# Two attention layers and two expert layers on one core: scores by array tiles of 32 rows, a new order around them, grouped row sums and reordered final adds

## The reference, cut to what matters

```
L0 attention:  q, k, v = x W + b, rotary on q and k, 16 heads of 8 channels
               softmax(q k^T / sqrt(8)) v, then Wo
L0 experts:    8 experts, each takes the 256 tokens with its highest probability
L1 attention:  q from x, k and v from a latent of 32 channels, 16 heads of 8
L1 experts:    16 experts, each token takes its best 4: weights softmax(top 4)
               sum over the 4 of  w * (gelu(x W1 + b1) W2 + b2)
```

## Time and profile before

| | us |
|---|---|
| median of three runs | 691.19 |
| the profiled execution | 691.12 |
| its span in the profile | 689.3 |
| PE busy / DVE busy / ACT busy / POOL busy | 540.6 / 493.6 / 385.9 / 326.8 |
| granted clock of TensorE, mean over the span | 0.882 |

### The profile page before, as it was taken

How to read it: one execution, slowest core, us unless ns; L and a number is a source line. 1 busy time by engine, 2 the same in 40 slices (tenths; PEclk the granted TensorE clock), 3 DMA queues, 4 the chain that set the end, 5 groups by cost and what they waited for, 6 DMA issues and landing times.

```text
span 689.3 us, 15558 instructions
## 1 busy us (share of the span) xinstructions
PE 540.6 (78%) x4528; PEld 388.7 (56%) x4528; DVE 493.6 (72%) x1779; ACT 385.9 (56%) x1004; POOL 326.8 (47%) x431
## 2 busy tenths in 40 slices
PE   4769999998512895378999999823899999999960
PEld 2224555555301785244555555512777899999960
DVE  6788888995576421868888899587577778863257
ACT  2348888886200564256888888530344555566633
POOL 5665555505001577562333330734344677777630
PEclk9689999999755799589999999955799999999985
DMA  6502080001100125336404000103334455555572
GB/s 185 160 1 71 9 232 24 1 1 41 26 0 3 39 49 101 122 94 178 136 11 123 1 2 1 47 16 105 119 126 136 156 185 177 177 194 203 199 249 77
DMA packets 64437, 65.08 MB, mean 94 GB/s; under 512 B 16115, under 2 KB 45955, under 8 KB 63846
## 3 DMA queue, kind: packets, MB, share of 16 engines
q1 hardware_dynamic: 57094, 52.49, 23.9%
q0 software_dynamic: 7264, 11.62, 6.9%
HBM read 29.77 MB, written 11.87 MB: 60 GB/s over the span
## 4 chain that ended last, share of the span: by engine, by line
PE 58%; DVE 22%; issue 6%; DMA 4%; POOL 4%; SPq 3%; ACT 2%; DVEq 0%; ACTq 0%; POOLq 0%
PE bank L1285 10%; PE bank L1296 9%; PE bank L898 8%; PE bank L865 8%; PE bank L881 7%; DVE mx L1687 2%; DVE passed L1887 2%; PE bank L915 2%; PE bank L1239 2%; PE bank L1080 1%; POOL rstd L711 1%; POOL sum L766 1%; PE bank L1266 1%; DVE keys L1737 1%; DVE stats L1831 1%
## 5 line engine op out<-in xcount | busy, mean ns | idle before, releaser
L1687 DVE TENSOR_REDUCE mx<-bank 128x2 f32<-128x512 f32 x256 | 166.2, 686 | 32.2 <-PE bank L865 29.3
L1406 ACT ACTIVATE prob<-bank 128x512 f32<-128x512 f32 x256 | 141.4, 597 | 45.4 <-PE bank L881 34.7
L1587 ACT ACTIVATE queries<-bank,prob 128x128 f32<-128x128 f32 x316 | 90.1, 368 | 81.3 <-PE bank L1285 80.5
L865 PE MATMUL bank<-keys,queries 128*128 128x512 f16 x256 | 99.3, 402 | 9.6 <-DVE queries L1747 4.0
L1285 PE MATMUL bank<-keys,prob 128*128 x632 | 90.0, 287 | 3.8 <-ACT keys L1579 3.7
L881 PE MATMUL bank<-QT,keys 128*128 128x256 f16 x512 | 90.3, 276 | 0.0
L1296 PE MATMUL bank<-W,queries 128*128 x632 | 87.8, 283 | 0.0
L1285 PEld LDWEIGHTS bank<-keys,prob 128*128 128x128 f32 x632 | 79.7, 198 | 8.8 <-issue 7.0
L779 POOL DMA_INDIRECT prob<-xs,idx_g x64 | 61.5, 961 | 46.4 <-DVE idx_g L2118 27.8
L1296 PEld LDWEIGHTS bank<-W,queries 128*128 128x128 f32 x632 | 77.6, 193 | 2.0
L898 PE MATMUL bank<-prob,augs 128*32 128x256 f32 x1024 | 77.2, 389 | 0.0
(11 more groups left out here) (272 smaller groups left out, 1021.4 us busy)
## 6 DMA issues: line engine op xcount, KB each, us to landing
prob<-W SPq DMA_DIRECT2D x79, 258.0 KB
W<-in_w SPq DMA_DIRECT2D x48, 256.0 KB, 3.5
sum<-zero SPq DMA_DIRECT2D x3, 1024.0 KB, 8.8
xr<-XT SPq DMA_DIRECT2D x12, 128.0 KB, 2.0
xs<-X SPq DMA_DIRECT2D x2, 768.0 KB, 6.2
prob<-xs,idx_g POOLq DMA_INDIRECT x80, 2.7
XB<-sum SPq DMA_DIRECT2D x1, 1024.0 KB, 5.3
Y<-sum SPq DMA_DIRECT2D x4, 256.0 KB, 4.8
```

The lines of the kernel that those rows point to most:

```text
L865: nc.tensor.matmul(bank[S1B[u % 2]][:, :], QT[par][:, j, P * qt:P * qt + P], KB[par][:, j, 2 * qp:2 * qp + 2, :], start=True, stop=True).t ...
L1406: nc.scalar.activation(prob[:, v % 8, :, :], st_bank(b, v)[:, :], ACT.Exp, scale=SCALE).then_inc(exp_done, 1)
L1587: last = nc.scalar.activation(hid2[:, p % 4, f, :], bank[2 + p % 2][:, P * f:P * f + P], ACT.Gelu, bias=wc[:, p % 4, WB + f:WB + f + 1])
L1687: nc.vector.tensor_reduce(m_at, bank[S1B[u % 2]][:, :].rearrange("p (j k) -> p j k", j=2), AX.X, ALU.max).then_inc(s1_used, 1)
```

## The change

- **Scores by row tiles.** `KB` goes. Keys are kept once, in `keyT`. A score matmul takes as operands only the 32 partitions of its head. `s1` is now two matmuls of 256 columns (heads of the same q in two groups) into one bank; unit u has q = u % 4. `st` is still two of 256.
- **Key evacuation by ACT alone**, two copies of 128x512 instead of four of 32x512 on ACT and four on DVE; one semaphore `kt_ready`. The memsets of `KB` go.
- **Order.** `soft_units`, and the places of `bt`, `av`, `front_proj`, `out_transposes`, `query_transposes` and `key_transposes` on PE; the matching places on ACT and DVE. `output_statistics` moves behind `m_ready`.
- **Experts of layer 1.** The expert number is computed once for each pair in the source. The sum L2130 is done for eight tiles at once.
- **Final adds.** Slice 1 to Y, bias to X, Y to X, then wait for slice 2 and add it to X.

```diff
 def soft_units(u):
-    return {2: [0, 1], 3: [2], 4: [3], 5: [4], 6: [5], 7: [6], 8: [7], 9: [8], 10: [9], 12: [10, 11],
-            14: [12], 15: [13]}.get(u, [])
+    return {2: [0], 3: [2], 4: [3], 6: [4, 5], 7: [6], 8: [7], 9: [8], 10: [9], 11: [10], 12: [11],
+            14: [12, 13]}.get(u, [])
...
 def s1(lay, i, par, u):
-    qt, j, qp = u // 8, (u % 8) // 2, u % 2
+    qt, jp, q = u // 8, (u % 8) // 4, u % 4
+    rows = slice(HP * q, HP * q + HP)
...
-    nc.tensor.matmul(bank[S1B[u % 2]][:, :], QT[par][:, j, P * qt:P * qt + P],
-                     KB[par][:, j, 2 * qp:2 * qp + 2, :], start=True, stop=True).then_inc(s1_done, 1)
+    for j in range(2):
+        last = nc.tensor.matmul(bank[S1B[u % 2]][:, L * j:L * j + L], QT[par][rows, 2 * jp + j, P * qt:P * qt + P],
+                                keyT[par][rows, 2 * jp + j, :], start=True, stop=True)
+    last.then_inc(s1_done, 1)
...
 def st(lay, b, par, v):
-                                KB[par][:, j, q, P * kt:P * kt + P], QT2[:, j, :],
+                                keyT[par][rows, j, P * kt:P * kt + P], QT2[rows, j, :],
...
 def pe_iteration(lay, i, par, soft_on, front_on, tail_on):
-        bt(lay, i - 2, 0)
     for u in range(16):
         s1(lay, i, par, u)
+        if u == 1 and tail_on:
+            bt(lay, i - 2, 0)
...
+        if u == 3 and soft_on:
+            st(lay, i - 1, nxt, 1)
...
+        if u == 7 + late and proj_on:
+            front_proj(lay, i + 2, par, 1)
+        if u in (10, 12) and soft_on:
+            av(lay, i - 1, nxt, 1, u // 12)
+        if u == 13 and tail_on:
             out_transposes(lay, i - 2)
         if u == 13 and front_on:
-            key_transposes(lay, i + 1, nxt)
+            query_transposes(lay, i + 1, nxt)
         if u == 15 and front_on:
-            query_transposes(lay, i + 1, nxt)
+            key_transposes(lay, i + 1, nxt)
-        if u == 12 and proj_on:
-            front_proj(lay, i + 2, par, 1)
...
 def keys_evac(lay, b, par, pair):   # ACT
-    for q in range(2):
...
-    last.then_inc(kb_act, 1)
+    nc.scalar.copy(keyT[par][:, 2 * pair:2 * pair + 2, :],
+                   half[M6][:, 2 * L * pair:2 * L * pair + 2 * L]).then_inc(kt_ready, 1)
...
 def dve_iteration(lay, i, par, front_on, tail_on):
-        if u == 11 and i > 2:
-            output_statistics(lay, i - 3)
         if u == 13 and front_on:
-            keys_evac(lay, i + 1, nxt, 0)
-        if u == 15 and front_on:
             q_evac(lay, i + 1, nxt)
...
-    if front_on:
-        keys_evac(lay, i + 1, nxt, 1)
+    if tail_on:
+        output_statistics(lay, i - 2)
...
 def row_owned(t):
...
+    if t % 8 < 7:
+        return
+    dve.wait_ge(own_ready, t + 1)
+    group = owned[:, t % RING - 7:t % RING + 1, 1, :]
-        nc.vector.tensor_reduce(idx_s[:, t:t + 1], owned[:, t % RING, 1, :], AX.X, ALU.add).then_inc(own_ready, 1)
+        nc.vector.tensor_reduce(idx_s[:, t - 7:t + 1], group, AX.X, ALU.add)
```

More of the change, by code:

```diff
@@ L367, in program @@
         rows_in = sem("rows_in")
-        own_step = sem("own_step")
         own_ready = sem("own_ready")
@@ L1451, in act_iteration @@
                 if soft_on:
-                    exps(lay, i - 1, (8, 9))
+                    exps(lay, i - 1, range(4, 9))
+                if proj_on:
+                    front_evac(lay, i + 2, par, 1)
+                if soft_on:
+                    exps(lay, i - 1, (9, 10, 11))
                 if tail_on:
@@ L1499, in keys_evac @@
                     act.wait_ge(st_done, 16 * (g - 2) + 8 * pair + 8)
-                for q in range(2):
-                    rows, js = slice(HP * q, HP * q + HP), slice(2 * pair, 2 * pair + 2)
-                    last = nc.scalar.copy(KB[par][rows, js, q, :],
-                                          half[M6][rows, 2 * L * pair:2 * L * pair + 2 * L].rearrange(
-                                              "p (j k) -> p j k", j=2))
-                last.then_inc(kb_act, 1)
+                nc.scalar.copy(keyT[par][:, 2 * pair:2 * pair + 2, :],
+                               half[M6][:, 2 * L * pair:2 * L * pair + 2 * L]).then_inc(kt_ready, 1)
             def front_evac(lay, b, par, t):
@@ L1727, in dve_last @@
                         norm(lay, i - 1, 0)
-            def keys_evac(lay, b, par, pair):
-                g = b + NB * lay
-                dve.wait_ge(tk_done, g + 1)
-                if not (isinstance(b, int) and g < 2):
-                    dve.wait_ge(st_done, 16 * (g - 2) + 8 * pair + 8)
-                for q in range(2, 4):
-                    rows, js = slice(HP * q, HP * q + HP), slice(2 * pair, 2 * pair + 2)
-                    last = nc.vector.tensor_copy(KB[par][rows, js, q, :],
-                                                 half[M6][rows, 2 * L * pair:2 * L * pair + 2 * L].rearrange(
-                                                     "p (j k) -> p j k", j=2))
-                last.then_inc(kb_dve, 1)
             def q_evac(lay, b, par):
@@ L2010, in choices_summed @@
                 dve.wait_ge(slice_back[0], 16)
-                for k in range(1, TOPK - 1):
-                    dve.wait_ge(slice_back[k], 16)
-                    for c in range(4):
-                        at = slice(4 * c, 4 * c + 4)
-                        last = nc.vector.tensor_tensor(Y[:, at, :], Y[:, at, :], slice_of[k][:, at, :], ALU.add)
-                    step(last)
+                dve.wait_ge(slice_back[1], 16)
                 for c in range(4):
                     at = slice(4 * c, 4 * c + 4)
-                    last = nc.vector.tensor_tensor(X[:, at, :], X[:, at, :], Y[:, at, :], ALU.add)
+                    last = nc.vector.tensor_tensor(Y[:, at, :], Y[:, at, :], slice_of[1][:, at, :], ALU.add)
                 step(last)
@@ L2025, in choices_summed @@
                                                    X[:, at, :], ALU.add)
+                step(last)
+                for c in range(4):
+                    at = slice(4 * c, 4 * c + 4)
+                    last = nc.vector.tensor_tensor(X[:, at, :], X[:, at, :], Y[:, at, :], ALU.add)
+                step(last)
+                dve.wait_ge(slice_back[2], 16)
+                for c in range(4):
+                    at = slice(4 * c, 4 * c + 4)
+                    last = nc.vector.tensor_tensor(X[:, at, :], X[:, at, :], slice_of[2][:, at, :], ALU.add)
                 step(last)
```

78 lines of the change are left out of this document (30 added, 48 removed).

## The result

The changed kernel takes 658.57 us (median of 4 runs, 655.67 to 659.00) where the kernel before takes 691.26 beside it: a ratio of 0.952, 95% interval 0.949 to 0.956. On another chip the comparison gave 656.98 against 691.38, 0.951 (0.948 to 0.955). The profiled execution took 658.15 us with a span of 656.3, against 691.12 and 689.3.

What follows compares the result with a forecast made beforehand. PE, DVE and ACT nearly filled, PE then DVE in the chain. Gains 23 (full iterations) + 4.4 (late iterations, last batch) + 3.6 (first iterations) + 3.5 (experts) + 2.3 (adds) = 36.8 us: 691.1 to 654.3 us, range 640 to 680 (own 645 to 666).

Steps and rivals of the forecast that it cites:

- no weight load of 107 ns: Score matmuls: the skill's load time, 107 ns whatever the rows, would cancel the overlap; the trace gave 0.056 us at most.
- the `mneg` step: Full iterations of layer 0: `mneg` falls from 0.88 to 0.17 us as POOL's rotary step ends earlier, gain 0.7 us.
- the earlier bias add in the first iteration: Layer 0, first iteration: POOL's bias add follows the second projection, now five units earlier; 2.8 us taken, at most 3.5.
- The rival in which the tiles do not overlap: Attention scores: row tiles do not run at once, full iterations take 16.3 and 16.8 us, total 675.6 us; chance 0.20.
- So DVE becomes the bound: Full attention iterations: DVE's 13.1 us of work plus 1.9 us idle gives 15.0 us, above PE's 13.9 us.
- Each join of two score units saves one slot of 0.109 us: PE in a full iteration: neighbouring score units overlap by one matmul; 23 joins save 2.5 us.
- 7 x 0.12 = 0.8 us: PE in a full iteration: added cost of switching between matmul forms, 21 groups counted instead of 7.
- the last batch: The batch behind the seventh iteration of each layer: a gain of 0.5 us a layer.
- the clock's fall: Attention: the granted PE clock drops, 0.75 in the example, as scores use a quarter of the rows; 711 us, chance 0.09.
- My own sign of being wrong: Forecast wrong if score units keep 0.22 us, a switch costs over 0.2 us, or the attention's clock is under 1.00.
- the experts: Layer 1's experts: grouped sums save 3.5 us (ends 0 and 4.8); the register instructions' 0.41 us idle stays.
- the end: Final adds: the 2.35 us wait for slice 2 is filled by other adds, gain 2.3 us.

Runs made afterwards that it cites:

- e2: The changed kernel with row tiles undone (128-row score matmuls, eight key copies, DVE's at the iteration's end): 1.018 of the kernel before.
- e3: The changed kernel plus twelve unread matmuls per layer (8 + 4) in two PE gaps of the last batch: 719.7 us, kernel before 750.6 (slower chip).
- e8: The changed kernel plus the same twelve unread matmuls per layer (8 + 4), run on a faster chip: 649.8 us, 0.938 of the kernel before.
- e1: The kernel before with row tiles for the score matmuls only, old order and all eight key copies: 1.026 of the kernel before (slower chip).
- e5: The kernel before with all 64 sums kept, each placed behind the marks of the next tile: 680.69 us, 0.986 of the kernel before.

## Why the prediction was right, and where it was not

**Right, with the mechanism as put.** That row tiles overlap; that no weight load of 107 ns stands in the way (the eight loads of the run above are recorded at about 0.10 us each, but start between 89.02 and 89.06 us, side by side); the `mneg` step; the earlier bias add in the first iteration; the clock of 1.00 in the full iterations i = 2 to 5. The rival in which the tiles do not overlap (675.6 us) fell with the timeline.

**Wrong: which engine bounds a full iteration.** "So DVE becomes the bound", with 13.1 us of work and 1.9 of waits, gave 15.0 us; it came out at 14.59 and 14.48. The chain of waits has no DVE in it: PE bounds the iteration with 13.1 us of its own, where I had 13.9, and 1.2 us of waits for ACT. The sum came near because the two engines' work is nearly alike.

**Mis-sized: the overlap.** "Each join of two score units saves one slot of 0.109 us" is too little: a run of four takes 0.33 us, not 0.55. "7 x 0.12 = 0.8 us" for the switches is too little too, 0.20 us each from row tiles to the full array. Together a full iteration came out 2.87 us shorter in layer 0 where 2.4 was forecast, and 2.77 in layer 1 where 2.2 was. That the first of the five, i = 1, gained only 0.6 and 0.9 us, at the slower clock, took most of the difference back, so 23 us stood against 23.9. What I did not see is that neither the tiles nor the order as tested in e2 would gain alone.

**Wrong: the last batch.** I gave it 1.0 us of gain and the clock's fall a chance of 0.09, in the full iterations. It fell behind them, where PE already had gaps, which the tiles made longer: 17.3 us lost there in place of 1.0 gained. The rival named the mechanism and not the place. My own sign of being wrong, a granted clock under 1.00 in the attention, came true here and in i = 1; that the total held in spite of it is luck.

**Wrong: the experts.** "The register instructions are the same four in both programs, so the 0.41 us ahead of the gate copy stays." It did not: those 0.41 us went with the wait for `own_step`. The term was 13.4 us, of which 11.0 belong to that wait. The end of the range that I gave the term, 4.8 us, excluded this: I had put the idle time at a fixed cost without a row for it.

**Mis-sized: the end,** 2.3 forecast, 1.2 in the first pair of traces, 1.5 to 2.2 over all runs.

The experts' 9.9 us too little and the last batch's 18.3 us too much leave 8.4; what the other stages gave beyond their terms takes 4.5 of these back, and the total was off by 4 us.

## What to carry to other kernels

Row tiles gain by runs, not by themselves: put units of all four row groups next to one another, for a run of four cost 0.34 us where a run of one cost 0.32, and count the crossings back to the full array at 0.20 us each. Alone, with another engine next in line, the tiles gained 0.06 us an iteration. When a faster engine will reach a wait sooner, ask what the clock does there: the time saved in a stretch with gaps was lost at 1.2 GHz over the next 20 us, and idle matmuls in the gaps were worth 7 us, though not in every execution. And read an "issue" idle ahead of an instruction with registers as a possible echo of the last semaphore wait before it on that engine: moving the waiting instruction one step later freed 11 us without removing anything.

## What the runs showed of the hardware

- Matmuls on different groups of 32 rows start within 0.02 us of one another, and a second one on the same rows 0.12 us later. Four score units side by side took 0.33 us where 0.88 were needed one after another.
- Once at 1.2 GHz the clock stayed there while PE was busy nearly throughout with this mixture of tiled and full matmuls: 151.3 to 163.3 us at 0.50 with 11.72 of 12 us busy. Full work did not bring it back in these 12 us.
- Of two profiled executions of one kernel (e3, e8), with the same idle time of 0.7 us in the same place, one kept the clock and one lost it, for 4.7 us. e1 with gaps of 1.63 and 0.82 us kept it in layer 0, and with 1.00 and 0.89 us lost it in layer 1.
- Register instructions behind a wait that is not yet over come late: 21.9 us of "issue" idle ahead of 79 gate copies, and 7.5 us with each waiting sum one step later (e5).
- The experts' stage moved 116 GB/s on one chip where the kernel with the same transfers moved 179 on another, while the attention's iterations were alike to 0.02 us. What a DVE edit is worth in this stage showed on the latter only.
